# Expert tiles of a retention block moved to fixed places in steps 8 to 28, the router weight applied ahead of the scatter, the output passes spread over the last steps

## The reference, cut to what matters

```python
xn = layernorm(x)                                  # x: 8 sequences of 512 tokens, 128 features
h = xn
for l in range(4):                                 # the retention stack
    k, q, v = split(h @ Wkqv[l], 3)
    r = tril(q @ k.T / sqrt(128)) / (1 + sqrt(arange(512)))[:, None]
    r = r / clip(abs(r.sum(-1)), 1)
    a, gate = split((r @ v) @ Wm1[l] + bm1[l], 2)
    m = groupnorm(a * silu(gate) @ Wm2[l] + bm2[l])    # one mean and variance for a sequence
    y = m + h
    h = layernorm(gelu(y @ Wf1[l] + bf1[l]) @ Wf2[l] + bf2[l] + y)
s = h
p = softmax(xn @ gate_w)                           # 8 experts, one chosen for a token
e, w = argmax(p), max(p)
y = w * (gelu(xn @ w1[e] + b1[e]) @ w2[e] + b2[e])
out = x + s * silu(y)
```

## Time and profile before

| what | us |
|---|---|
| median of 3 runs (lowest, highest) | 517.68 (517.53, 518.33) |
| the profiled execution's own time | 517.43 |
| its span on the core | 515.4 |
| PE busy | 469.9 |
| DVE busy | 386.7 |
| ACT busy | 261.5 |
| POOL busy | 251.6 |

### The profile page before, as it was taken

How to read it: one execution, slowest core, us unless ns; L and a number is a source line. 1 busy time by engine, 2 the same in 40 slices (tenths; PEclk the granted TensorE clock), 3 DMA queues, 4 the chain that set the end, 5 groups by cost and what they waited for, 6 DMA issues and landing times.

```text
span 515.4 us, 9900 instructions
## 1 busy us (share of the span) xinstructions
PE 469.9 (91%) x3179; PEld 393.7 (76%) x3179; DVE 386.7 (75%) x1342; ACT 261.5 (51%) x561; POOL 251.6 (49%) x304
## 2 busy tenths in 40 slices
PE   7999899999999999999999999999999999999400
PEld 5887666667888898888898888988889888886300
DVE  4768888878777777866777777787767777777896
ACT  3822434444566565454556565655555565665710
POOL 4570288887444443345444344434454443444663
PEclk9998999999999999999999999999999999999955
DMA  9999611113211011111011110111011010105014
GB/s 256 233 142 190 204 36 37 36 38 68 58 58 63 32 58 37 35 61 63 29 40 58 33 63 31 58 42 59 31 63 40 30 58 31 63 33 150 25 41 122
DMA packets 48833, 36.16 MB, mean 70 GB/s; under 512 B 13960, under 2 KB 39888, under 8 KB 48784
## 3 DMA queue, kind: packets, MB, share of 16 engines
q1 hardware_dynamic: 45824, 29.73, 22.5%
q0 software_dynamic: 2432, 5.02, 3.4%
q10 hardware_dynamic: 528, 0.79, 0.5%
HBM read 14.85 MB, written 9.84 MB: 48 GB/s over the span
## 4 chain that ended last, share of the span: by engine, by line
PE 71%; POOL 10%; DVE 8%; issue 5%; DMA 2%; ACT 1%; SPq 0%; DVEq 0%; POOLq 0%
PE bank L1290 9%; PE bank L1219 7%; PE bank L1199 7%; POOL x_slots L494 6%; PE pair L1335 5%; PE pair L1359 4%; PE pair L1317 4%; PE bank L1372 4%; PE bank L1230 4%; PE bank L1231 4%; PE bank L1232 4%; PE pair L1315 3%; PE pair L1361 3%; PE bank L1255 3%; PE bank L1288 2%
## 5 line engine op out<-in xcount | busy, mean ns | idle before, releaser
L517 POOL TENSOR_TENSOR zhat<-zhat,all_lg 128x512 f32<-128x512 f32 x31 | 40.6, 1309 | 96.0 <-PE bank L1264 95.7
L1290 PE MATMUL bank<-all_f,G_sb 128*128 128x128 f32 x512 | 72.9, 275 | 0.0
L712 ACT ACTIVATE y_sb<-bank,gn_bi,gn_sc 128x512 f32<-128x512 f32 x32 | 24.9, 778 | 94.3 <-DVE gn_bi L1055 94.3
L707 ACT ACTIVATE uT_h<-bank 128x512 fp32r<-128x512 f32 x32 | 19.1, 597 | 99.6 <-PE bank L1274 99.6
L564 POOL DMA_INDIRECT y_rows<-yt,tile_ids x39 | 40.3, 1033 | 58.1 <-DVE yt L1101 51.4
L1290 PEld LDWEIGHTS bank<-all_f,G_sb 128*128 128x128 f32 x512 | 67.4, 192 | 1.4 <-issue 1.4
L1199 PEld LDWEIGHTS bank<-moe_w,h_T 128*128 128x128 f32 x312 | 39.7, 191 | 14.6 <-issue 14.6
L450 POOL TENSOR_TENSOR ln_rs<-ln_ve,half_neg 128x4 f32<-128x4 f32 x32 | 33.1, 1035 | 29.4 <-DVE ln_ve L736 29.1
L618 ACT ACTIVATE h_T<-bank,w_t 128x128 f32<-128x128 f32 x156 | 44.6, 375 | 4.6 <-PE bank L1219 4.6
L1219 PE MATMUL bank<-xtT,w_t 128*128 128x128 f32 x320 | 44.6, 282 | 0.1
L689 ACT ACTIVATE G_sb<-bank,all_par 128x512 f32<-128x512 f32 x64 | 42.6, 703 | 1.7
(11 more groups left out here) (181 smaller groups left out, 1243.3 us busy)
## 6 DMA issues: line engine op xcount, KB each, us to landing
w_t<-moe_w SPq DMA_DIRECT2D x41, 258.0 KB, 2.3
xt<-x_slots SPq DMA_DIRECT2D x41, 65.0 KB, 1.8
x_slots<-moe_w SPq DMA_DIRECT2D x1, 2644.5 KB
x_sb<-in_L_attn_x SPq DMA_DIRECT2D x8, 256.0 KB, 6.0
moe_w<-in_L_ffn_w SPq DMA_DIRECT2D x1, 2048.0 KB, 19.1
moe_w<-y_rows SPq DMA_DIRECT2D x8, 256.0 KB, 4.7
out<-moe_w SPq DMA_DIRECT2D x8, 256.0 KB, 2.2
all_f<-in_L_attn_Wf SPq DMA_DIRECT2D x2, 512.0 KB, 5.3
```

What stands on the lines that cost most here:

```text
L517: pool.tensor_tensor(zhat[:, b % 2, :, :], zhat[:, b % 2, :, :], all_lg[:, li, :].unsqueeze(1).broadcast_to([P, C, D]), ALU.mult)\
L1290: last = mm(bank[7][:, at_c], G_sb[:, k, at_c], all_f2[:, li, k, :], start=False, stop=k == 1)
```

## The change

The tile count falls from 41 to 39 (the two padding tiles at the end are gone), the 41 turns stand at fixed places: two in step 7, then EARLY and LATE in every step up to 28, but for steps 8, 15 and 22, which have LATE alone. Steps 29 to 31 have no turn. The last two turns are partial: turn 39 transposes nothing, turn 40 makes only the last second product. Tiles use rings of five buffers, loaded up to four turns ahead.

Half the router weight travels with the token's row number through `x_slots`; POOL multiplies each finished tile with it ahead of the scatter, so that `weigh` at the end goes and ACT's tanh becomes one instruction for a sequence. POOL no longer copies the row numbers of a tile, and the five scatters of zeros in step 1 (`first_rows`) go.

In the last layer the transposes of zhat and ACT's hT, which nothing reads, go for blocks 24 to 30; POOL's `htok` passes then wait for zhat itself. The tanh passes stand in steps 30, 31 and 32, the `silu_y` passes at the ends of these steps, and all `times_s` and `add_x` passes are DVE's: sequences 0 to 2 in step 31, 3 in step 32, 4 to 6 in step 33. `finish_last` works in two halves, each with its own output transfer. In step 32 PE makes the means ahead of G.

```diff
-        TURNS = [[LATE] if t in (0, 3, 5) else [EARLY, LATE] for t in range(B)]
+        PLACES = [(s, place) for s in range(B - 1, LB) for place in (EARLY, LATE)
+                  if not (place == EARLY and s in (B, B + 7, B + 14))][:TURNS]
...
+        TANH_AT = {LB - 2: (0, 1, 2), LB - 1: (3, 4, 5), LB: (6, 7)}
+        SILU_AT = {LB - 2: (0, 1, 2), LB - 1: (3, 4, 5), LB: (6, 7)}
+        OUT_AT = {LB - 1: (0, 1, 2), LB: (3,), LB + 1: (4, 5)}
...
 # POOL, tile_rows
-                pool.wait_ge(yt_out[q], 16 * (1 + used_before(l, k)))
-                pool.tensor_copy(tile_ids[q][:, :], slot_ids[:, bass.ds(j - TILE_LAG, 1)]).then_inc(ids_set, 1)
...
+                pool.wait_ge(yt_done, i + 1)
+                pool.tensor_scalar(yt[ring(i)][:, :], yt[ring(i)][:, :], slot_info[:, i, 1:2], None, ALU.mult)\
+                    .then_inc(yt_weighed, 1)
+                pool.wait_ge(yt_weighed, i + 1)
...
 # POOL, the htok passes
-                    pool.wait_ge(pe_zT, n + 1)
+                    if n < LAST_LAYER:
+                        pool.wait_ge(pe_zT, n + 1)
+                    else:
+                        pool.wait_ge(z_done, n + 1)
...
 # DVE
+            def outputs(bs):
+                for b in bs:
+                    dve.wait_ge(e_silu, b + 1)
+                    dve.wait_ge(htok_done, LB - B + b + 1)
+                    y = y_tok[:, b, :].rearrange("p (c d) -> p c d", c=C)
+                    dve.tensor_tensor(y, y, tokens(htok, b), ALU.mult).then_inc(e_s, 1)
+                for b in bs:
+                    dve.wait_ge(e_s, b + 1)
+                    y = y_tok[:, b, :].rearrange("p (c d) -> p c d", c=C)
+                    dve.tensor_tensor(y, y, tokens(x_sb, b), ALU.add).then_inc(dve_out, 1)
...
                 for stage in (gn_moments, split_u) if first and 2 <= t < B - 1 else (split_u, gn_moments):
                     stage(l, t)
+                if l * B + t in (LB - 1, LB + 1):
+                    outputs(OUT_AT[l * B + t])
+                if l * B + t == LB + 1:
+                    prepare_last()
                 if w := at(l, t, 2, B, LB):
                     dve.wait_ge(pe_z, w[0] + 1)
                     ln_stats(w[0], w[1])
...
+                for b in SILU_AT.get(l * B + t, ()):
+                    silu_y(b)
+                if l * B + t == LB:
+                    outputs(OUT_AT[LB])
+                if l * B + t == LB + 1:
                     finish_last()
...
 # PE
-                if w and w[0] != LB - 1:
+                if w and w[0] < LAST_LAYER:            # zhat_by_feature; the same in ACT's hT
...
-                              (u_by_feature, gelu_second, means)):
+                              (means, gelu_second) if l == L else (u_by_feature, gelu_second, means)):
```

More of the change, by code:

```diff
@@ L288, in parted, with turned @@
+        def turned(count):
+            return min(count, TILES)
         def parted(l, t):
-            return turn(l, t, EARLY) is not None and not (l == 0)
+            return turn(l, t, EARLY) is not None and l > 0
         def parted_steps(l, t):
-            early = [k for k in range(B) if EARLY in TURNS[k]]
-            return (l - 1) * len(early) + early.index(t) + 1
+            return sum(parted(k // B, k % B) for k in range(l * B + t + 1))
         def halves(l, t):
             return (0, 1) if parted(l, t) else (1, 0)
-        def first_turns(j):
-            return isinstance(j, int) and j < TILE_LAG
@@ L1033, in step @@
                     find_experts()
-                if ends and t == 1:
-                    prepare_last()
-                    for b in (0, 1):
-                        times_s(b)
-                        add_x(b)
-                    for b in (2, 3):
-                        silu_y(b)
                 tile_out(l, t, LATE)
@@ L1193, in tile_back @@
-                if w is None or first_turns(w[0]):
+                j = turn(l, t, place)
+                if j is None or j < TILE_LAG:
                     return
-                j, k = w
+                i = j - TILE_LAG
                 e = loaded[place]
-                pe.wait_ge(h_done, j - 1)
-                for i in range(KF):
-                    last = mm(bank[5][:, 0:D], h_T[:, i * P:(i + 1) * P],
-                              moe_w2[:, bass.ds(e, 1), i, :].rearrange("p a d -> p (a d)"),
-                              start=i == 0, stop=i == KF - 1)
+                pe.wait_ge(h_done, i + 1)
@@ L1202, in tile_back @@
+                for k in range(KF):
+                    last = mm(bank[5][:, 0:D], h_T[:, k * P:(k + 1) * P],
+                              moe_w2[:, bass.ds(e, 1), k, :].rearrange("p a d -> p (a d)"),
+                              start=k == 0, stop=k == KF - 1)
                 last.then_inc(pe_y, 1)
             def tile_front(l, t, place, gelu_read):
-                w = turn(l, t, place)
-                if w is None:
+                j = turn(l, t, place)
+                if j is None:
@@ L1259, in zhat_by_feature @@
                 w = at(l, t, 3, B, LB)
[L1260 removed]
+                if w and w[0] < LAST_LAYER:
                     n, b, _ = w
```

349 lines of the change are left out of this document (133 added, 216 removed).

## The result

The changed kernel takes **514.94 us** (median of eight runs, 512.11 to 517.25) where the kernel before takes 517.48: ratio 0.995, interval 0.9926 to 0.9975. It is half a percent faster, and the forecast of 519.8 had the wrong sign, though the time lies inside its range. A second measurement on another chip gave 515.78 (twelve runs, 512.46 to 519.60), ratio 0.9961 (0.9942 to 0.9979). The kernel before spreads over 1 us and this one over 5 to 7, and that spread turned out to hold most of the answer. Three executions that took far longer (one of e5 with 696 us, two of the kernel before with 1262 and 1700) are left out throughout.

A forecast was written before the change was run, and what follows sets the result against it. PE bounds two-turn steps, the engine chain turnless ones, DVE the drain's last third. +6.1 for steps 8 to 28, -2.3 for 29 to 31, then 46.1 us instead of 47.5 gave 519.8 us, range 513.3 to 523.5.

The forecast's parts named there:

- Steps 8 to 28, +6.1: Five steps get a second turn, +8.15; dropped padding-tile work -1.19 and zhat transposes -0.88; step 29 begins at 432.1.
- The weighing, 0: POOL's multiplication of each tile by its weight in steps 8 to 28: taken as 0, at most 0.40 us a tile.
- Steps 29 to 31: Steps of 12.3, 12.3 and 14.8 us, -2.3 in all; moments of block 30 read (R) at 471.7.
- my 2.5: Three silu_y passes ending step 30, the third meeting POOL's first htok pass, delay u: +2.5 us.
- the collision of step 32: POOL's two htok passes fall on the third silu_y and on L978; w2 starts at R + 14.1.
- Rival 2: Drain: no collisions where forecast, passes shifting by tenths; removes 6.2, 513.6 us; chance 0.15, plus 0.06 with the clock staying.
- its third part: Step 33: sequence 3 passes beside POOL's htok passes without a collision; 2.6 of the 6.2 us removed.
- the means: Step 32: the means stand ahead of G on PE; half clock adds 0.15 us to them.
- the passes behind y_done: VectorE's passes from y_done of block 31 to VectorE's end: 16.5 us.
- The clock, +3.2: Drain: PE's clock falls to half in its waits; w2 +0.85, means +0.15, G +2.2.
- stays: Drain: once fallen ahead of w2, PE's clock remains at half, 1.2 GHz; w2 +0.85.
- The end, 4.4 behind VectorE: From VectorE's end to the span's end: 4.4 us, taken from the kernel before, a little less for half the size.

The follow-up runs named there:

- e5: The changed kernel with POOL's htok passes of step 32 waiting for VectorE's gated passes of that step; 516.69 us (515.58 to 517.23).
- f3: e9's kernel with GpSimd multiplying each of the 39 tiles by its weights twice; 521.71 us (521.20 to 522.15).
- e9: The changed kernel with POOL's htok passes waiting for the gated passes in both steps 31 and 32; 514.51 us (514.18 to 514.84).
- f6: The changed kernel as it is, measured again on another chip; 515.78 us (512.46 to 519.60).
- e1: The changed kernel with 27 constant products put into PE's waits in steps 31 to 33; 514.63 us (512.11 to 515.93).
- e2: The changed kernel with the six output passes of sequences 0 to 2 moved from step 31 to step 32; 514.15 us (513.25 to 515.11).
- e3: The changed kernel with both the constant products of e1 and the moved output passes of e2; 512.50 us (512.00 to 512.82), ratio 0.9909.
- e7: e4's kernel with the last sequence finished in whole passes and one transfer instead of halves; 514.27 us (514.12 to 514.55).
- e10: e4's kernel with one small memset more on POOL near the end, which nobody waits for; 515.80 us (514.58 to 516.96).
- e11: e4's kernel with POOL's last ln_rs made by a ScalarE square root and a VectorE reciprocal; 511.73 us (511.21 to 513.48), ratio 0.9897.
- f2: e9's kernel with all eight silu_y and the outputs of sequences 0 to 3 at the end of step 32; 513.01 us (511.98 to 513.18).
- e4: The changed kernel with the last layer's zhat transposes and hT put back, POOL's htok passes waiting for the transposes; 514.30 us (514.04 to 514.51).
- f4: f5's kernel with step 33's VectorE passes in one row, POOL's last two passes behind it, sequence 6 last; 507.66 us, ratio 0.9805.
- f1: The changed kernel with POOL's htok passes waiting for VectorE's gated passes in step 31 only; 516.47 us (514.85 to 517.17).
- e12: The changed kernel with constant products, moved output passes, POOL behind the gated passes in steps 31 and 32, and e11's root; 508.79 us (508.71 to 509.99).
- f5: The kernel of e12 again, on the same chip as f4; 508.59 us (508.31 to 508.73).

## Why the prediction was wrong

*Steps 8 to 28, +6.1*: right but for 0.6; step 27 took 15.16, since TensorE waited 0.52 there for xtT.

*The weighing, 0*: right, with its cover (0.66 of idle time ahead of `gn_rs`); the upper bound of 0.40 us a tile was too low, 0.606. The nearest row had been a cast, and the bound should have gone further. f3 shows what stood behind the cover.

*Steps 29 to 31*: 12.22 for each of the first two against 12.3, and R at 471.62 against 471.7. But R was right by luck: step 29 began 0.6 late, and the third step, which I gave 14.8, took 14.31 from moments to moments. Those 14.8 contained a collision on a `silu_y`, and the profiled execution had none, only the held gated pass of 1.65 us. Without any collision the step takes 13.97 (e9), so the three passes cost 1.75 us; with one on a `silu_y` it takes 16.41 and R is 473.6 (f6; e5 alike), since TensorE waits 2.77 us for A_sb instead of 1.71 and drops to half clock. Passes and collision together, 4.2, are far above my 2.5.

*The step that failed* is the collision of step 32, "POOL's two htok passes fall on the third and on L978". I took the collision for certain and by its worst order. The rows show an exclusion, in which one of the two is held and the other is not. The Trainium skill ("SBUF — State Buffer", "Who interferes with whom") calls the ports that the two engines share an exclusive lock and says that the order of issue decides who blocks. Here POOL started 0.20 us ahead of the third `silu_y`, while the one before it still ran for 0.28, and did not always get in; where page and rows differ the rows decide. If VectorE keeps it, the loss falls on POOL, for whose passes nobody on the path waits.

The case of 519.60 has both collisions lost; that it is my forecast to 0.2 us is partly luck, for R came 1.9 late and the drain behind y_done of block 31 was 1.8 shorter than I had it. 514.47 is the same kernel with VectorE first in both, and the median lies between. Rival 2, which I gave 0.21, has the right size for step 32 but not the mechanism: the passes do not shift past each other, they meet always, and I had not weighed which of them waits; its third part, sequence 3 without a collision, did not come (1.64 and 1.76 us for two VectorE passes at 496.22 and 497.78). From w2 on the collision is -2.8 of the miss of 5.4 in the span; the clock and the means are some -0.7, the passes behind y_done -0.7, the end -1.1.

*The clock, +3.2*: G at half, +2.2, as forecast; in the execution of 514.47 it came back to full for w2 (-0.85), so "stays" was wrong there, while in that of 519.60 w2 took 2.08 at half clock. As a lever it moves the median little alone (e1) and 1.65 us on top of e2's edit (e3 against e2).

*The end, 4.4 behind VectorE*: 3.3, -1.1. The size came from VectorE's end before, and VectorE was not what it hangs on. Of the halves, which I priced, e7 shows nothing; what the end hangs on is POOL's last instruction, at 506.29 here (e10 moved it, e11 took it away). In the kernel before, POOL's last were three output passes, over at 508.85, and the end was 6.5 us behind them.

*Why it is faster at all*: not by the spreading (f2), nor by the missing transposes (e4). By the forecast's own terms, steps 8 to 31 lose 3.7 and the rest wins 6.7 in the profiled execution. Of the rest, the drain no longer has the eight `weigh` passes and three `add_x` passes on POOL, beside which VectorE's passes took up to 1.64 us in place of 0.68, and the end comes sooner behind VectorE. The kernel before, POOL and then DVE:

```profile
482.80 4.31 POOL L501 TENSOR_TENSOR moe_w<-moe_w,half_w 128x512 f32<-128x512 f32 x3 [1.80 <-DVE moe_w L896]
...
503.87 4.98 POOL L506 TENSOR_TENSOR moe_w<-moe_w,x_sb 128x512 f32<-128x512 f32 x3 [1.23 <-DVE moe_w L903]
```

```profile
484.69 1.52 DVE L916 TENSOR_TENSOR xn<-moe_w,all_lg 128x512 f32<-128x512 f32 x1
...
507.76 1.64 DVE L908 TENSOR_TENSOR moe_w<-moe_w,x_sb 128x512 f32<-128x512 f32 x1
```

I did not take that part back by itself, so this split is read from rows and not shown.

## What to carry over

When two engines share an access, ask which of them will wait, and who waits for that one; if the answer hangs on 0.2 us, forecast both cases and expect a spread. One wait that fixes the order (two lines, e9) took it from 5 us to 0.7, and with the order fixed the last plan of the drain (f4) was met to 0.5 us. Before pricing the last transfer, look what the end of the span really follows.

## What the runs showed of the hardware

- Beside a row of VectorE passes without a wait a GpSimd pass of 128x512 lasted 12.84 us (f2) and 2.61 us (f1, the changed kernel); it takes 1.27 alone. In f2 and in the changed kernel it ended 1.12 us behind the first pause in the row after its start, one of 0.04 us. In the execution of 519.60 it got into such a row without a pause (1.41 us), and a power on 128x1 ended inside a row in both executions of the changed kernel (0.94 us instead of 0.55, at 472.31 and 474.29), so a row does not keep every instruction out every time.
- A VectorE instruction on 128x4 with two SBUF operands was held as well, 0.85 us instead of 0.16 (f4).
- The span ended 6.13 us behind GpSimd's last instruction in fifteen profiles, 6.53 in the kernel before, and 0.42 us behind the last landing where that was later (e11, e12, f4, f5).
- TensorE's clock fell to half at 465.45, inside a wait of 2.8 us for A_sb (f6), and at 478.38, at the end of one of 5.1 us for y_sb (the changed kernel). There it came back for single stretches, at 481.79 behind f1 and at 502.27 behind G, and TensorE did little in these stretches themselves (1.50 and 0.18 us of 3.41).
- A square root on ScalarE (0.20 us, its table loaded ahead in 1.28) and a reciprocal on VectorE (0.17) stood in for a power on GpSimd of 1.40 (e11); the gain was in the closing and not in `ln_nb`.
